# B's rows spread by transfers in place of TensorE, with new shares for TensorE and GpSimd in a Mamba scan that runs beside a gated FFN

## The reference, cut to what matters

```python
def _L0_ffn_ref(x, w_gate_up, w_proj):
    gu = einsum('bsd,hd->bsh', x, wq_gu)            # wq_gu, wq_p: ternary_quant of the weights
    gate, up = split(gu, 2, axis=-1)
    h = silu(gate) * up
    hn = rms_norm(h)
    return einsum('bsh,dh->bsd', hn, wq_p)

def step(state, xs):                                # one token of the scan; 256 channels, 16 states
    d_t, B_t, C_t, u_t = xs
    dA = exp(d_t[..., None] * A)
    state = state * dA + (d_t * u_t)[..., None] * B_t[:, None, :]
    y_t = einsum('ben,bn->be', state, C_t)
    return (state, y_t)
```

## Time and profile before

| | us |
|---|---|
| median of 3 runs | 470.47 (466.97 to 470.56) |
| the profiled execution's own time | 469.82 |
| its span, from the first to the last instruction | 468.1 |
| busy in the span: PE, DVE, ACT, POOL | 347.9, 337.2, 227.9, 320.5 |

### The profile page before, as it was taken

How to read it: one execution, slowest core, us unless ns; L and a number is a source line. 1 busy time by engine, 2 the same in 40 slices (tenths; PEclk the granted TensorE clock), 3 DMA queues, 4 the chain that set the end, 5 groups by cost and what they waited for, 6 DMA issues and landing times.

```text
span 468.1 us, 6613 instructions
## 1 busy us (share of the span) xinstructions
PE 347.9 (74%) x1799; PEld 238.8 (51%) x1809; DVE 337.2 (72%) x772; ACT 227.9 (49%) x443; POOL 320.5 (68%) x231
## 2 busy tenths in 40 slices
PE   4819924689988899888266267989788888798870
PEld 3414812244444454444156156777676766676650
DVE  3999799899999889999786955555444554454464
ACT  1999959686886877873422002333222322222210
POOL 3112638599999999999420364887887878887860
PEclk9977765899999989999855567999998999999995
DMA  8900004166566323322000243889888888865558
GB/s 249 378 13 7 1 0 132 55 185 194 183 221 195 128 103 131 128 102 90 0 0 1 113 113 82 212 214 220 192 200 191 204 206 204 218 147 91 95 67 267
DMA packets 53929, 64.72 MB, mean 138 GB/s; under 512 B 5586, under 2 KB 42242, under 8 KB 53778
## 3 DMA queue, kind: packets, MB, share of 16 engines
q1 hardware_dynamic: 42752, 47.59, 32.4%
q0 software_dynamic: 9984, 16.78, 18.7%
q10 hardware_dynamic: 1170, 0.08, 0.2%
HBM read 53.36 MB, written 11.08 MB: 138 GB/s over the span
## 4 chain that ended last, share of the span: by engine, by line
POOL 33%; PE 19%; DVE 14%; issue 11%; DMA 10%; ACT 10%; another core or an unknown queue 1%; SPq 1%; DVEq 0%; POOLq 0%; ACTq 0%
POOL ssm L561 11%; POOL ssm L566 6%; POOL sums L621 6%; PE bank L1166 5%; DMA ssm<-routed,idx 5%; PE bank L1150 3%; POOL ssm L610 3%; POOL ffn L572 3%; PE bank L1144 3%; PE bank L1131 3%; DMA arena<-in_L_ffn_w_gate_up 2%; DMA sums<-ssm,idx 2%; PE bank L1093 2%; DVE x_res L1402 2%; DVE bank L1366 1%
## 5 line engine op out<-in xcount | busy, mean ns | idle before, releaser
L621 POOL DMA_INDIRECT sums<-ssm,idx x48 | 78.7, 1640 | 21.6 <-issue 13.6
L1471 DVE COPY ssm<-bank 128x256 f32<-128x256 f32 x64 | 27.1, 424 | 80.2 <-PE bank L1131 64.6
L610 POOL DMA_INDIRECT ssm<-routed,idx x64 | 65.8, 1028 | 26.6 <-issue 16.1
L561 POOL TENSOR_TENSOR ssm<-ssm,bc_buf 128x1024 f32<-128x1024 f32 (+1 forms) x33 | 76.0, 2304 | 8.0 <-DVE ssm L1371 5.7
L1371 DVE TENSOR_TENSOR_SCAN ssm<-ssm,bank 128x512 f32<-128x512 f32 x64 | 78.1, 1221 | 4.6 <-POOL ssm L561 2.3
L1166 PE MATMUL bank<-arena,ssm 128*128 (+1 forms) x256 | 57.5, 349 | 7.5 <-issue 3.9
L862 ACT ACTIVATE ssm<-bank 128x96 f32<-128x96 f32 x64 | 16.0, 250 | 88.6 <-PE bank L1166 77.4
L1150 PE MATMUL bank<-ssm,xin 128*128 128x256 bf16 x384 | 51.9, 274 | 0.1
L1166 PEld LDWEIGHTS bank<-arena,ssm 128*128 128x128 f32 x256 | 42.2, 199 | 14.4 <-issue 11.4
L855 ACT ACTIVATE ssm<-bank 128x256 f32<-128x256 f32 x64 | 24.5, 383 | 51.3 <-PE bank L1144 36.1
L1131 PE MATMUL bank<-ident,ssm 128*128 128x128 f32 x128 | 28.6, 307 | 21.5 <-DMA ssm<-routed,idx 21.3
(11 more groups left out here) (215 smaller groups left out, 687.1 us busy)
## 6 DMA issues: line engine op xcount, KB each, us to landing
bc_buf<-c_rows SPq DMA_DIRECT2D x32, 512.0 KB, 3.7
arena<-in_L_ffn_gate_proj SPq DMA_DIRECT2D x32, 192.0 KB
arena<-in_L_ffn_up_proj SPq DMA_DIRECT2D x32, 192.0 KB
arena<-in_L_ffn_down_proj SPq DMA_DIRECT2D x32, 192.0 KB
sums<-zero_f SPq DMA_DIRECT2D x1, 2304.0 KB, 14.1
arena<-in_L_ffn_w_gate_up SPq DMA_DIRECT2D x1, 2048.0 KB, 11.4
routed<-xw SPq DMA_DIRECT2D x1, 1280.0 KB, 4.4
x_res<-in_x SPq DMA_DIRECT2D x1, 1024.0 KB, 7.0
```

The source lines that it names most:

```text
L561: pool.tensor_tensor(prod[:, a:b, :], hs[:, a:b, :], C_buf[:, a:b, :], ALU.mult).then_inc(s.prod_ok, 1)
L610: pool.indirect_dma_start(out=xe[:, k, :], out_offset=None, in_=routed, in_offset=bass.IndirectOffsetOnAxis(ap=idx2[:, k, 0:1], axis=0)).t ...
L621: pool.indirect_dma_start(out=sums, out_offset=bass.IndirectOffsetOnAxis(ap=idx2[:, k, 1:2], axis=0), in_=ye[:, k, :], in_offset=None, com ...
```

## The change

1. **B by transfers.** The head stores B's 16 rows beside C's (`bc_rows`), and SP spreads two rows at a time over the partitions (`b_load`, 512 KB a pair, three buffers `B_buf`). The matmuls `broadcast`, `sel`, `B_parts` and what made them go.
2. **du in bank 5.** ACT copies the phase's tile of du into PSUM bank 5 (`keep_du`), for the first phase in the head, for the three later ones in units 3, 7 and 11, where it waits for the last mult of the phase. mult now reads bank 5 and a tile of `B_buf`, and writes bank 6 or 4.
3. **PE adds all products** in two of three units (four matmuls, two early in the unit and two late). Units 2, 5, 8, 11 and 14 (`PAIRED`) keep `add_pairs` and two matmuls.
4. **POOL makes the FFN's product** (`pool_hidden`) in units outside `ON_DVE` (the paired ones and the last); as POOL reads no PSUM, ACT copies up into `up_sb` behind the silu.
5. **Order.** On POOL, `add_square(f - 1)` moves from between the unit's two products to behind the second one and behind `add_pairs`. On ACT, the square of an unpaired unit moves into the next unit, ahead of its silu; that of a paired unit stays two decays behind the silu's unit. The experts' loads are spread over 16 units.

```diff
+PAIRED = tuple(f for f in range(UNITS) if f % 3 == 2)
+ON_DVE = PAIRED + (UNITS - 1,)
...
+            def b_load(q):
+                if q >= 2:
+                    sp.wait_ge(ld_B[q % 2], 16 * (q // 2))
+                if q >= 3:
+                    sp.wait_ge(s.dBu_ok, 2 * q - 4)
+                sp.dma_start(B_buf[q % 3], rows(q, DS)).then_inc(ld_B[q % 2], 16)
             def c_load(q):
...
+                if q >= 2:
+                    sp.wait_ge(s.prod_ok, q - 1)
+                sp.dma_start(C_buf[:, 2 * (q % 2):2 * (q % 2) + 2, :], rows(q, 0)).then_inc(ld_C[q % 2], 16)
...
             for f in range(UNITS):
-                if f < PRE // 2:
+                if f % 2 == 0 and f < PRE:
                     sp.wait_ge(s.quantT_ps, 6)
-                    moe_load(f % 2, 2 * f)
+                    moe_load((f // 2) % 2, f)
...
+            def pool_hidden(f):
+                pool.wait_ge(s.silu_ok, silus_before(f + 1))
+                if f > 1:
+                    pool.wait_ge(s.hsq_ok, f - 1)
+                    pool.wait_ge(s.proj_ok, f - 1)
+                pool.tensor_tensor(hT[f % 2], gate_sb, up_sb, ALU.mult).then_inc(s.h_ok, 1)
...
             for f in range(UNITS - 1):
                 product(2 * f)
+                if f not in ON_DVE:
+                    pool_hidden(f)
+                product(2 * f + 1)
+                if f in PAIRED:
+                    add_pairs(f)
                 if f > 0:
                     add_square(f - 1)
                 if f == 9:
                     rms(0)
-                product(2 * f + 1)
-                add_pairs(f)
...
+            def keep_du(p):
+                if p == 0:
+                    act.wait_ge(s.quantT_sb, 1)
+                    act.wait_ge(s.du_sb, 1)
+                else:
+                    act.wait_ge(s.dBu_ok, DS * p)
+                if p == 1:
+                    act.wait_ge(s.du_sb, 2)
+                act.activation(bank[5][:, :], du[:, p % 2, (p // 2) * 512:(p // 2) * 512 + 512], ACT.Copy).then_inc(s.du_ps, 1)
...
+            def square(f):
+                act.wait_ge(s.h_ok, f + 1)
+                if f > 0:
+                    act.wait_ge(s.acc_ok, f + 2)
+                act.activation(hsq, hT[f % 2], ACT.Square).then_inc(s.hsq_ok, 1)
...
                 decay(4 * f + 2)
                 decay(4 * f + 3)
+                if f > 0 and f - 1 not in ON_DVE:
+                    square(f - 1)
                 act.wait_ge(s.gu_ps, f + 1)
                 act.activation(gate_sb, bank[7][:, :], ACT.Silu).then_inc(s.silu_ok, 1)
-                for k in (4 * f + 4, 4 * f + 5):
-                    if k < STEPS:
-                        decay(k)
-                act.wait_ge(s.h_ok, f + 1)
-                if f > 0:
-                    act.wait_ge(s.acc_ok, f + 2)
-                act.activation(hsq, hT[f % 2], ACT.Square).then_inc(s.hsq_ok, 1)
+                if f not in ON_DVE:
+                    act.activation(up_sb, bank[0][:, :], ACT.Copy).then_inc(s.silu_ok, 1)
+                if 4 * f + 4 < STEPS:
+                    decay(4 * f + 4)
                 if f and f % 4 == 0:
                     keep_y(f // 4 - 1)
+                if 4 * f + 5 < STEPS:
+                    decay(4 * f + 5)
+                if f % 4 == 3 and f + 1 < UNITS:
+                    keep_du(f // 4 + 1)
+                if f in ON_DVE:
+                    square(f)
...
             for f in range(UNITS):
-                broadcast(4 * f + 2)
                 gate_up(f)
...
-                broadcast(4 * f + 3)
-                if 4 * f + 4 < STEPS:
-                    broadcast(4 * f + 4)
+                if f > 0:
+                    sum_late(f - 1)
                 if f == 9:
                     pe.wait_ge(s.po_copy, 2)
                     squares(0, bank[1])
                 elif f > 0:
                     project(f - 1)
-                if f > 0:
-                    sum_pairs(f - 1)
-                if 4 * f + 5 < STEPS:
-                    broadcast(4 * f + 5)
+                if f not in PAIRED:
+                    sum_early(f)
...
-                x = bank[(5, 6, 4)[k % NB]]
-                dve.wait_ge(s.bb_ps, k + 1)
-                dve.tensor_tensor(x[:, :], du[:, h, t], x[:, :], ALU.mult).then_inc(s.dBu_ok, 1)
+                x, q = bank[(6, 4)[k % 2]], k // 2
+                if k % DS == 0:
+                    dve.wait_ge(s.du_ps, k // DS + 1)
+                dve.wait_ge(ld_B[q % 2], 16 * (q // 2 + 1))
+                if k >= 2:
+                    dve.wait_ge(s.scan_ok, k - 1)
+                dve.tensor_tensor(x[:, :], bank[5][:, :], B_buf[q % 3][:, k % 2, :], ALU.mult).then_inc(s.dBu_ok, 1)
```

131 lines of the change are left out of this document (62 added, 69 removed).

## The result

| | before | after |
|---|---|---|
| median of 6 runs, side by side (us) | 469.88 (466.97 to 471.62) | 485.7 (485.23 to 486.5) |
| ratio, 95% interval | | 1.0355 [1.0318, 1.0391] |
| the profiled execution | 469.82 | 485.95 |
| its span | 468.1 | 484.2 |

The kernel got 3.5% slower, where 486.6 us was forecast.

A forecast was written before the change was run, and what follows sets the result against it. POOL alone was taken to bound the kernel, 8.5 us a unit. In the new order waits put the last scan 19.6 us later, the statistics 17.4; less 0.6 in the head, +16.8 on 469.8 gives 486.6 us, eight in ten 474 to 497.

The forecast's parts named there:

- the walk: Loop, followed wait by wait over three units: a group takes 28.8 us against 25.5 before; chance 0.75.
- the ring: Loop's chain of scan, product, (pairs), addition of the square, ACT's square, decay, scan; scan(4f+6) loses 3.3 us behind paired units.
- Three groups hold a `keep_du`, I take 1.0 for each: Loop, units 3, 7 and 11: the copy of du adds 1.0 us to each group, with 0 and 1.9 as ends.
- a short fall would be hidden: PE's clock in the loop: only a lasting half clock costs +3.5 us a group; a short one costs nothing.
- rival D: PE in paired units: idle some 4 us, its clock falls to half, +3.5 us a group, 500 us; chance 0.03.
- 0.6 won: Head: without POOL's copies of B, one DVE operation on the chain takes 0.69 us instead of 1.30.
- Scan(11) 0.5 won: Loop's start: scan(11), unit 2's last, ends at 106.6 us instead of 107.1.
- Some is given back: Behind the loop: the last scan is 19.6 us later, but the point behind the statistics only 17.4 later.
- by busy time alone a unit could fall to 7.6 us: Loop: the engines' summed work, without waits, would allow 7.6 us a unit; DVE's sum is 22.8 us for three.
- C: Transfers in the loop: rows land late with B's traffic added, 495 us; chance 0.07.
- A: Loop: waits stay hidden and busy time decides, 22.8 instead of 25.5 us for three units, 456 us; chance 0.08.
- B: Loop: only each group's first wait tells, 26.1 us for 25.5, 472 us, within 1%; chance 0.07.

The follow-up runs named there:

- run 1: The kernel after, with POOL's addition of the square back between the unit's two products: 472.52 us, 1.0085 of the kernel before.
- run 2: The kernel after, order kept, with two buffers for the squares instead of one: 471.26 us, 1.0047 of the kernel before.
- run 5: The kernel before, with POOL's addition of the square moved behind the second product and the addition of pairs in every unit: 527.42 us, 1.1212.
- run 3: The kernel after, with ACT's squares of the paired units moved into the next unit, ahead of its silu: 479.57 us, 1.0244 of the kernel before.
- run 6: The kernel after, with B's rows loaded for the first three pairs only and old rows used later: 488.04 us, 1.0366 of the kernel before.
- run 12: run 10 with the addition of the square behind the second product, as in the kernel after: 479.01 us, 1.0134 of the kernel before.
- run 7: run 1 with B's rows loaded for the first three pairs only and old rows used later: 473.91 us, 1.0057 of the kernel before.
- run 10: run 8 with the FFN's product back on POOL in two of three units: 465.39 us, 0.9846 of the kernel before.
- run 8: The kernel after without pairs (PE adds all products), FFN's product on DVE everywhere, addition of the square between the products: 464.45 us, 0.9866 of before.

## Why the prediction was right, and where it was off

The ends of scans below are the starts in the timeline plus 1.22 us. A group is three units, from the end of one paired unit's last scan to that of the next.

| | predicted | measured after |
|---|---|---|
| end of scan 11 | 106.6 | 108.09 |
| group of unit 2 (with `keep_du`), to scan 23 | 29.8 | 31.4 |
| group of unit 5 (with `keep_du`), to scan 35 | 29.8 | 29.7 |
| group of unit 8 (forecast with the third `keep_du`), to scan 47 | 29.8 | 29.6 |
| group of unit 11, to scan 59 | 28.8 | 28.9 |
| from there to the last scan | 12.5 | 12.6 |
| last scan | 237.3 | 240.26 |
| statistics behind the loop | 243.2 (+17.4) | 245.65 (+19.9) |
| whole execution | 486.6 | 485.95 |

- **The walk of a group was right**, step by step: 28.8 us was forecast for a group without a `keep_du`, and the last one took 28.9. In units 2, 5 and 14 scan 4f+6 starts 7.54 or 7.55 us after the unit's last scan, where the walk has 7.6, having waited 3.26, 3.27 and 3.25 us (3.3 predicted). Unit 11's wait is 2.58, but its scan 4f+6 starts as late (7.54): 0.58 us of it were spent before, at a mult that waited for `keep_du`. The sum of the scans' waits is 23.4 us (20 to 25 predicted), though 2.76 of it lie at scan 4, before any paired unit. The 36.8 us for the squares ("nearly 40"), the 5.9 for the mults behind `keep_du` ("4 to 6") and a chain that alternates were right too. The small additions on POOL became no cheaper (1.27 us each, as before), so the end of the range at 478 had nothing behind it.
- **The cause was right, and shown**: runs 1 and 2 break the ring in two different places and leave 1.0085 and 1.0047; run 5 puts it into the old kernel and loses 12%.
- **"Three groups hold a `keep_du`, I take 1.0 for each"** was undersized in the first. That group took 1.6 us more than forecast. `keep_du` itself came as in the walk (the mult waited 3.02 us for it, and the next scan starts 14.4 us after scan 11's end, 14.5 in the walk). Behind it came a step that the walk left out: PE's sums of unit 4 wait for `keep_y`, in a group whose ACT is late, and run at the low clock.

```profile
129.28 0.58 ACT L833 ACTIVATE bc_buf<-bank 128x512 f32<-128x512 f32 x1
...
130.00 3.51 PE L1041 MATMUL bank<-ssm,ident 128*128 128x512 f32 x4 [2.94 <-ACT bc_buf L833]
...
133.30 2.94 PE L1092 MATMUL bank<-xs,wguT 128*128 128x512 bf16 x12
...
136.28 0.60 ACT L856 ACTIVATE ffn<-bank 128x512 f32<-128x512 f32 x1 [1.34 <-PE bank L1092]
```

  The silu was 1.34 us late for PE, and DVE's FFN product ahead of the group's last scan waited 2.17 us for it. So "a short fall would be hidden" held in the other groups, not in this one; rival D was at work here in small.
- **The third `keep_du` was put where it cost nothing, and another copy took its place.** It delays scan 48, behind scan 47, so it belongs to the group of unit 11, and there it is hidden (28.9 us all the same). The group of unit 8 is 0.8 us longer than 28.8 for another reason: in unit 8 ACT copies the projection out of PSUM (L839, 1.06 us) between the late square and the decays, so that scan 38 waits 4.22 us, the longest wait of all. The walk has no such copy. That the group comes out at 29.6 for 29.8 is luck.

```profile
175.92 1.06 ACT L839 ACTIVATE xw<-bank 128x512 f32<-128x512 f32 x2
...
177.69 1.22 DVE L1418 TENSOR_TENSOR_SCAN ssm<-ssm,bank 128x512 f32<-128x512 f32 x1 [4.22 <-issue]
```

- **"0.6 won" in the head** can't be seen in the whole. The operation on DVE did fall from 1.30 to 0.69 us, but the first scan starts at 82.30, 0.34 later than before (81.96). DVE is already 0.7 us later long before these rows (a reduction that starts at 32.02 before starts at 32.76 now), and run 3, whose head is the same as that of the kernel after, has its first scan 1.4 us earlier. A term of 0.6 is smaller than what one profile can tell there.
- **"Scan(11) 0.5 won"** failed: it ended 1.0 later than before. The first silu started at 89.20, not 87.92, as it waited 3.63 us for a `gate_up` that ran at the low clock (5.28 us for its 12 matmuls). Up to there runs 3, 6 and 12 do what the kernel after does (run 6 without most of B's transfers), and their scan 11 ends at 106.1, 107.7 and 107.6. So the 1.5 us between 106.6 and 108.1 are within what one profile can say.
- **"Some is given back"** was right, and larger: from the last scan to the statistics 5.4 us, against 8.1 before. L1450, which is L1402 of before, took 3.72 us instead of 5.67; POOL was busy beside it for 2.7 us in place of 5.4.
- **Two errors cancel in the total.** The loop cost about 3 us more than forecast. The experts' stage, from the first gather to the end, took 200.0 us before and 196.2 after, and the change touches no instruction of it. It isn't a gain: over the profiles of this study it lies between 196.2 and 201.5, and run 6, whose code there is the same, has 198.4. The medians, +15.8 us, are the better measure of the change, and the forecast of +16.1 on the median owes part of its closeness to this.
- **What failed as a reading:** "by busy time alone a unit could fall to 7.6 us" (its term for POOL in a paired unit, 8.4, is 8.25 when added up, which changes nothing here, as DVE's sum is the larger). With the ring opened (run 1) it didn't: the loss went from 3.5% to 0.9%, not to a gain. The walk followed PE only as far as its own clock; it didn't ask what is queued behind the pairs on PE when the rest gets faster. The pairs in one unit of three cost 10 to 11 us in either order (the table of run 12), so the change carries two costs of like size, and I had named one. That the pairs cost it through PE's idle 2.2 to 3.3 us and what stands behind is read from the timeline of run 1, not tested apart from the clock: how much of the 11 us is the gap and how much the slower matmuls behind it stays open.
- **The rivals.** C falls by runs 6 and 7 for B's transfers, and POOL waits for none of C's in the kernel after. A and B fall by the scans' waits: A has none behind a paired unit, B none but the first, and behind units 5, 8 and 11 there is a second one of 1.3 to 1.4 us, at decay(4f+8), as the walk has it. Part 4 is neutral (run 10 beside run 8), and parts 1 to 3 together, with all products on PE, are the gain (run 8) that the order and the pairs hide.

## What to carry to other kernels

Before an instruction is moved on an engine that isn't waiting, list who waits for it and through which single buffer: a wait of 2 us that cost nothing here became one of 6.2 us that cost 13 us in all, and in the old kernel 56. A second buffer for the squares (256 KB and a few lines) took that ring away as well as the old order did. And where a plan mixes two ways of doing a thing (pairs here, PE there), try each alone: here the mixture stopped PE for 2.2 to 4.0 us in each third unit, and all on PE was faster than either kernel.
